# Attention denominators: one small reciprocal between two TensorE transposes, or four wide reciprocals in place in PSUM

## The reference, cut to what matters

```python
x = q                                    # (4, 1024, 128) float32
xn = layernorm(x)
xq, xk, xv = rope(xn @ Wq), rope(xn @ Wk), xn @ Wv      # 16 heads of 64, k and v from 8 x 64 repeated
xk, xv = repeat(xk, 2, axis=-1), repeat(xv, 2, axis=-1)
scores = softmax(xq @ xk * 0.5, axis=-1)                # (4, 16, 1024, 1024)
attn = (scores @ xv) @ Wo
ffn = (silu(xn' @ w_gate.T) * (xn' @ w_up.T)) @ w_down.T  # xn' = xn, weights are int8-like * 1/127
out = x + attn + ffn
```

## Time and profile before

| what | value |
|---|---|
| median of three runs | 1212.84 us |
| profiled execution / its span | 1210.01 / 1208.2 us |
| PE busy (matmuls) / PEld | 1161.2 us (96%) / 642.0 us (53%) |
| DVE | 892.1 us (74%) |
| ACT | 697.7 us (58%) |
| POOL | 878.2 us (73%) |
| mean granted TensorE clock | 0.989 of full speed |

### The profile page before, as it was taken

One profiled execution on the slowest core, in us unless ns is written; L12 is line 12 of the kernel. 1 busy time (PEld: TensorE's weight loads), 2 busy tenths in 40 slices (PEclk: granted clock), 3 DMA queues, 4 the chain that ended last, 5 costly groups with the idle time before them and its releaser, 6 DMA issues.

```text
span 1208.2 us, 19402 instructions
## 1 busy us (share of the span) xinstructions
PE 1161.2 (96%) x6288; PEld 642.0 (53%) x6288; DVE 892.1 (74%) x1009; ACT 697.7 (58%) x1074; POOL 878.2 (73%) x274
## 2 busy tenths in 40 slices
PE   5898999999999999999999999999999999999985
PEld 4786455555555555555555555555555555554432
DVE  7685778777777778777777777777777777876622
ACT  3333556666666656666666656666666556665563
POOL 2312777887778877787777887787777887787775
PEclk9898999999999999999999999999999999999997
DMA  6652707062421517062422517061422517050000
GB/s 222 172 238 99 213 2 217 1 188 65 142 76 62 156 36 215 0 197 55 141 75 74 143 36 215 0 202 49 148 68 87 131 36 215 0 125 1 4 1 17
DMA packets 56287, 124.58 MB, mean 103 GB/s; under 512 B 7968, under 2 KB 19488, under 8 KB 54048
## 3 DMA queue, kind: packets, MB, share of 16 engines
q1 hardware_dynamic: 56224, 123.89, 35.0%
HBM read 53.08 MB, written 10.49 MB: 53 GB/s over the span
## 4 chain that ended last, share of the span: by engine, by line
PE 90%; DVE 3%; POOL 2%; ACT 1%; issue 1%; DMA 1%; SPq 1%; POOLq 0%; ACTq 0%; DVEq 0%
PE bank_s L542 24%; PE scores L379 22%; PE bank_o L394 20%; PE scores L362 7%; PE bank_m L370 3%; PE bank_m L404 3%; PE bank_m L430 2%; PE bank_m L407 2%; POOL prob_sum L1018 2%; PE scores L480 2%; PE bank_s L497 1%; PE bank_m L414 1%; PE bank_m L421 1%; DVE prob L917 1%; DMA x_all<-x 1%
## 5 line engine op out<-in xcount | busy, mean ns | idle before, releaser
L824 DVE TENSOR_REDUCE row_max<-scores 128x1 f32<-128x1024 f32 x512 | 605.7, 1217 | 194.7 <-PE scores L379 194.7
L1018 POOL TENSOR_TENSOR prob_sum<-prob_sum,prob 128x2048 f32<-128x2048 f32 x128 | 586.3, 4581 | 112.9 <-DVE prob L917 103.8
L542 PE MATMUL bank_s<-qk_pack 98*128 98x512 f32 x1024 | 383.6, 432 | 12.8 <-ACT prob L768 6.7
L779 ACT ACTIVATE prob<-bank_s 128x512 f32<-128x512 f32 x512 | 285.1, 596 | 172.3 <-PE bank_s L542 165.1
L768 ACT ACTIVATE prob<-bank_s 128x1024 f32<-128x1024 f32 x256 | 262.5, 1025 | 187.8 <-PE bank_s L542 180.5
L379 PE MATMUL scores<-qk_pack 96*128 96x512 f32 x1024 | 340.5, 419 | 1.1 <-DVE row_max L824 1.1
L542 PEld LDWEIGHTS bank_s<-qk_pack 98*128 98x128 f32 x1024 | 183.0, 189 | 232.4 <-ACT prob L768 144.3
L394 PE MATMUL bank_o<-prob,v 128*32 128x512 f32 x2048 | 273.6, 606 | 0.9 <-ACT prob L779 0.9
L379 PEld LDWEIGHTS scores<-qk_pack 96*128 96x128 f32 x1024 | 177.0, 190 | 136.8 <-DVE row_max L824 109.1
L963 POOL TENSOR_TENSOR qk_stage<-rope,qk_stage 128x512 fp32r<-128x512 f32 x64 | 82.1, 1283 | 90.8 <-ACT qk_stage L653 90.8
L1011 POOL TENSOR_TENSOR prob_sum<-prob 128x2048 f32<-128x2048 f32 x32 | 146.4, 4575 | 0.0
(11 more groups left out here) (88 smaller groups left out, 679.5 us busy)
## 6 DMA issues: line engine op xcount, KB each, us to landing
qk_pack<-qk_stage SPq DMA_DIRECT2D x384, 128.0 KB, 3.5
table<-tables SPq DMA_DIRECT2D x16, 2048.0 KB, 9.9
w_stage<-w_scratch SPq DMA_DIRECT2D x14, 640.0 KB, 4.7
v<-v_stage SPq DMA_DIRECT2D x32, 256.0 KB, 3.2
xT_scratch<-xT_hl SPq DMA_DIRECT2D x4, 1024.0 KB, 9.5
x_stage<-xT_scratch SPq DMA_DIRECT2D x4, 1024.0 KB, 5.4
w_scratch<-w_split SPq DMA_DIRECT2D x1, 2560.0 KB, 15.1
x_all<-x SPq DMA_DIRECT2D x4, 512.0 KB, 12.5
```

Of the source, the lines that this page charges most:

```text
L542: mm(bank_s[:, h % 2, :], qk_pack[j][0:SCORE_K, 1, kt // QT, h, (kt % QT) * 128:(kt % QT + 1) * 128], qk_pack[j][0:SCORE_K, 0, t, h, :], s ...
L779: A(prob[:, kt % RING, h, :], bank_s[:, h % 2, :], ACT.Exp).then_inc(prob_ready, 1)
L824: V.tensor_reduce(row_max[:, m:m + 1], scores[:, at:at + 2, :].rearrange("p c k -> p (c k)"), axis=AX.X, op=ALU.max).then_inc(max_read, 1)
L1018: TT(prob_sum[:, t], prob_sum[:, t], prob[:, kt % RING], ALU.add).then_inc(sum_done, 1)
```

## The change

The reciprocal is taken of all 32 copies, in `bank_m` itself, by DVE: four instructions of 128 columns on 128 partitions instead of one of 16. They stand behind the row-maximum tiles m9, m10, m11 and m12. The two ACT copies, the two sets of four PE transposes, the tile `den_inv` and four semaphores are gone. The end of `denominators` now releases DVE itself, and `normalise` waits for its four reciprocals.

```diff
-INVERT_AFTER = 13
+INVERT_AFTER = [9, 10, 11, 12]
...
-            def transpose_den(u):
-                pe.wait_ge(den_read, u + 1)
...
-            def transpose_inv(u):
-                pe.wait_ge(inv_spread, u + 1)
...
                     elif kt == 4:
-                        if not is_first(u):
-                            transpose_den(u - 1)
                         maxima()
-                    elif kt == 5:
-                        if not is_first(u):
-                            transpose_inv(u - 1)
...
-            def read_den(u):
...
-            def spread_inv(u):
...
-            def invert(u):
-                dve.wait_ge(denT_ready, u + 1)
-                V.reciprocal(den_inv[:], bank_m[:].rearrange("p (j h e) -> p j h e", j=QT, h=HG)[:, :, :, 0]).then_inc(inv_done, 1)
+            def invert(u, k):
+                cols = slice(k * 128, (k + 1) * 128)
+                dve.wait_ge(den_ready, u + 1)
+                V.reciprocal(bank_m[:, cols], bank_m[:, cols]).then_inc(inv_done, 1)
 
             def normalise(u):
-                dve.wait_ge(inv_ready, u + 1)
+                dve.wait_ge(inv_done, QT * (u + 1))
...
-                        if m == INVERT_AFTER and not is_first(u):
-                            invert(u - 1)
+                        if m in INVERT_AFTER and not is_first(u):
+                            invert(u - 1, m - INVERT_AFTER[0])
                     split_max(u + 1)
                 else:
-                    invert(u - 1)
+                    for k in range(QT):
+                        invert(u - 1, k)
```

More of the change, by code:

```diff
@@ L111, in build @@
         den = keep("den", [128, HALF])
-        den_inv = keep("den_inv", [128, QT, HG])
         y_part = keep("y_part", [128, HALF])
@@ L178, in build @@
             sem("prob_ready"), sem("pv_done"), sem("pair_done"), sem("sum_done"), sem("den_ready"))
-        o_read, den_read, denT_ready, inv_done, inv_spread, inv_ready = (sem("o_read"), sem("den_read"),
-            sem("denT_ready"), sem("inv_done"), sem("inv_spread"), sem("inv_ready"))
+        o_read, inv_done = sem("o_read"), sem("inv_done")
         o_done, y_ready, y_read, y_added = sem("o_done"), sem("y_ready"), sem("y_read"), sem("y_added")
@@ L408, in denominators @@
                 last.then_inc(den_ready, 1)
-            def transpose_den(u):
-                pe.wait_ge(den_read, u + 1)
-                for j in range(QT):
-                    last = nc.tensor.transpose(bank_m[:, j * 128:(j + 1) * 128], den[:, j * 128:(j + 1) * 128], ident[:])
-                last.then_inc(denT_ready, 1)
-            def transpose_inv(u):
-                pe.wait_ge(inv_spread, u + 1)
-                for j in range(QT):
-                    last = nc.tensor.transpose(bank_m[:, j * 128:(j + 1) * 128], den[:, j * 128:(j + 1) * 128], ident[:])
-                last.then_inc(inv_ready, 1)
             def project_out(u, n, s):
@@ L630, in _ @@
             denominators(UNITS - 1, 1)
-            transpose_den(UNITS - 1)
-            transpose_inv(UNITS - 1)
             project_out(UNITS - 1, 1, STEPS - 1)
@@ L728, in read_o @@
                 nc.scalar.copy(o_raw[:], bank_o[:]).then_inc(o_read, 1)
-            def read_den(u):
-                act.wait_ge(den_ready, u + 1)
-                at_least(act, inv_ready, u)
-                nc.scalar.copy(den[:], bank_m[:]).then_inc(den_read, 1)
-            def spread_inv(u):
-                act.wait_ge(inv_done, u + 1)
-                nc.scalar.copy(den[:].rearrange("p (j h e) -> p j h e", j=QT, h=HG),
-                               den_inv[:].unsqueeze(3).to_broadcast([128, QT, HG, E])).then_inc(inv_spread, 1)
             def read_y(u):
@@ L774, in slot @@
                         read_y(u - 2)
-                    elif kt == 5 and not first:
-                        spread_inv(u - 1)
                     for h in (2, 3):
@@ L783, in slot @@
                         round_hi(1, u + 3, 1 - t, s + 1 + t)
-                    elif kt == 2 and not first:
-                        read_den(u - 1)
                     elif kt == 6 and not (last_pair and j == 1 and t == 1):
@@ L799, in _ @@
             read_y(UNITS - 2)
-            read_den(UNITS - 1)
-            spread_inv(UNITS - 1)
             read_y(UNITS - 1)
@@ L951, in _ @@
             pairs_of_steps(dve, body)
-            invert(UNITS - 1)
+            for k in range(QT):
+                invert(UNITS - 1, k)
             normalise(UNITS - 1)
```

## The result

The changed kernel takes 1257.49 us, the median of four runs (1255.74 to 1258.19), against 1212.42 us for the kernel before in four runs beside it: a ratio of 1.037, 95% interval 1.0352 to 1.0388. Its profiled execution has a span of 1253.9 us, 45.7 more than before. The forecast was 1250.7 us with a range of 1230 to 1273.

What follows compares the result with a forecast made beforehand. It took PE, chained to ACT and to DVE's tiles, as the bound; 30 units x 1.28 us less 0.5 gave 1247.9 us profiled, and with 2.8 for the median 1250.7 us, range 1238 to 1264 (68%), 1230 to 1273 (80%).

Steps and rivals of the forecast that it cites:

- What bounds the kernel: Middle units: PE, 33.88 of 33.90 us busy, tied to ACT's exponentials and DVE's tiles; DVE seems to have 7.5 us left.
- (a): The eight PE transposes removed, four ahead of m14's load and four ahead of a wait for ACT: at most 0.3 us a unit.
- (b): The two ACT copies removed, L734 and L739: neither lies ahead of something late, so nothing is gained.
- The reciprocal's price: On DVE, 128 columns take 0.95 us, carried on from three narrow reciprocals at 6.25 ns a column; each moves what follows 0.86.
- The walk: One unit followed from m9's end: three reciprocals make PE's load of m14 late, by 1.28 us a unit.
- Nothing is added elsewhere: Behind m14, through project(0), the normalisation and POOL's cushion, no further loss arises and nothing takes the 1.28 us back.
- The sum: Whole program: 30 units x 1.28 = 38.4 us, less 0.5 at the end; profiled time from 1210.0 to 1247.9 us.
- 1 (dearer column): DVE's reciprocals cost more per column beyond 24: 1271.7 us, or 1343 at the proportional bound; 12% together.
- 3 (mostly fixed cost): Reciprocals under 0.52 us end PE's wait ahead of m14, so not slower: down to 1203 us; 6%.
- 2 (clock): PE's clock falls in the new gap of about 1.2 us ahead of m14: 2.8 us more a unit, 1335 us; 6%.
- 4 (half absorbed): PE's catching up on ACT's chain leaves half the lateness, 0.65 us a unit: 1231 us; 8%.
- Signs: Expected in the profile: DVE up 114 us to some 83%, units of 35.2 us, full clock in the middle, m14 released by DVE.

Runs made afterwards that it cites:

- e4_spread: Changed kernel with PE's code moved by 16 tiny matmuls, its four wide reciprocals behind tiles m9, m12, m13 and m15 instead of m9 to m12: 1214.62 us, ratio 1.0025.
- e3_narrow: Changed kernel with PE's code moved by 16 tiny matmuls, each reciprocal over only the first 16 of its 128 columns: 1203.85 us, ratio 0.9927.
- e5_log: Changed kernel with PE's code moved, DVE's reciprocals replaced by logarithm and exponential on ACT in the old copies' places: 1206.22 us, ratio 0.9967.
- e1_shift: Changed kernel with 16 unused tiny matmuls ahead of PE's first wait for weights, moving later PE code by 64 instructions: 1241.55 us, ratio 1.0239.
- e6_late: Changed kernel with PE's code moved by 16 tiny matmuls, its four wide reciprocals behind tiles m12, m13, m14 and m15: 1240.09 us, ratio 1.0242.

## Why the prediction was right, point by point

- **What bounds the kernel.** Right: PE, tied to DVE tile by tile and to ACT score by score. DVE's free 7.5 us a unit lie in small gaps, of 0.46 to 1.48 us in the rows. e4_spread shows what that means: spread over them, the same 3.4 us cost 0.25 us a unit instead of 1.27.
- **(a) and (b), what goes.** "At most 0.3 us a unit": 0.20 (e3_narrow). That the copies are worth nothing is borne out by e5_log, which keeps two ACT operations of their length and has the same unit within 0.02 us.
- **The reciprocal's price.** 0.95 us: measured 0.949.
- **The walk.** Place, order and engine were right; 1.28 us was over by 0.25, since a unit grew by 1.03. The term that was mis-sized is a tile that stands behind a reciprocal. It was put at 1.22 us, with 1.14 to the start of what follows. All 120 such tiles of the changed kernel's trace take 1.16 us, and the next reciprocal starts 1.08 us after the tile did (411.48 to 412.56). Tiles that stand behind another tile do start 1.14 us apart. Three times 0.06 is 0.18, and m14's load is 0.19 less late than forecast. The row for it was there: 1.16 at 507.27, behind the small reciprocal. The remaining 0.06 is made up between m14 and the next normalisation. Over 30 units 0.25 is some 7 us too much.
- **"Nothing is added elsewhere".** Wrong, by 15.1 us, and by more than the walk's error in the other direction. The sum was 37.9, the trace has 30.6 without and 45.7 with the long units. The prediction asked what the removed instructions free on PE, and not where the code behind them comes to lie. That the median landed only 7 us above the forecast is in part luck: two errors partly cancel. With the code moved (e1_shift, 1241.55 us) the forecast is 9 us too high, and the range holds too.
- **Rivals.** 1 (dearer column): 6.23 ns a column from 16 to 128 (251, 551, 749, 949 ns), so no. 3 (mostly fixed cost): falls with the same numbers; the time that it named for a cheap reciprocal, 1203, is what e3_narrow takes (1203.85). 2 (clock): not in the gap ahead of m14, where the prediction looked for it, but behind two returns of PE's loop, and in e6_late. Its price was read too low: after 113.87 the clock of the kernel before stays at 0.50 until 120.5 us, 6.6 us and not 5.6. 4 (half absorbed): no, in e1_shift 1.07 of a gross 1.27 stays, and the other 0.20 is what the removed steps give back.
- **Signs.** DVE was to reach 83%; it has 78% (975.7 us, 83.6 more, where 114 were forecast). The reciprocals add 113 us as forecast; the rest is split's first step, which falls from 488 ns to 0.17 us where it no longer waits ahead of its work (420.74 in the unit above), shorter tiles (599.6 us instead of 605.7), and starts that overlap the row before, which busy time counts once. The unit was to be 35.2 us and is 34.92. The clock was to be full in the middle and was not, twice. The load of m14 came 0.06 us after m12 was read, as forecast.

Left open: how the place of the loop decides whether it is fetched again, why a return then makes PE wait once in one kernel and twice in another, behind which waits the clock falls, and why the knee between 16 and 96 columns is soft.

## What to carry to other kernels

A dependence of an engine in order on another, tile by tile, makes small gaps the currency: put added work into the gaps that the timeline shows, not into the share of idle time. Carry the price of an operation on from two narrow forms of it in the trace, if there are such. And after an edit that changes how many instructions stand ahead of or in a long loop, read the instruction queue's packets before explaining the time: here 16 us, over a third of the loss, had nothing to do with the edit's work. Where the units of a loop differ, ask for the granted clock in a window of a few microseconds: the slices of the page average a short fall away.

## What the runs showed of the hardware

- A VectorE reciprocal in PSUM costs 6.23 ns a column in float32, 949 ns for 128x128. That is 5.7 times the column of an addition or multiplication here (1.09 ns, from L819 with 512 columns in 692 ns and L917 with 2048 in 2364).
- A reduction of 128x1024 from PSUM takes 1160 ns behind a reciprocal, 1215 behind another reduction and 1224 after a pause (medians, kernel before).
- A PE loop can fetch its whole code again in each pass (9 packets of 16 KB, three of them at the return) or not at all, by its place: a move of 64 instructions switched this off in the changed kernel, one of 128 switched it on in the kernel before, and one of 64 there did nothing. A return costs 1.2 to 2.9 us then at the full clock.
- Behind such waits of 1.0 to 1.5 us the granted clock fell to 0.50 at seven of fifteen returns, and the units with it were 0.8 to 3.4 us longer than those without.
- ScalarE takes Ln from PSUM in 597 and Exp from SBUF in 622 ns for 128x512, within 13 ns of its copies.
- A pause of PE of 0.65 us, behind one of 0.46 us, was followed by the lower clock in e6_late, in every sixth unit, and not in the units between with pauses of 0.46 to 0.65 us at the same place.
